# Late weights in 20 pieces behind the key quarters, and query transposes spread one by one, in a two-layer Perceiver kernel

## Chip, cores and metric

One core of one Trainium2 chip runs the whole program in one launch. The metric is the device time of that core in microseconds, the median of three runs. All engines of the core work side by side: PE (matrix products), DVE and ACT (vector and scalar work), POOL (small vector work), and SP, which here only issues DMAs.

## The reference, cut to what matters

The input is a sequence of 256 rows of 256 values and a context of 4096 rows. Two layers follow each other, each with a cross attention over the context, a self attention and a feed-forward part, every part added to x.

```python
x = x + L0_xattn(layernorm(x), ctx, ctx, mask)      # 16 heads of 16, tanh-capped scores
x = x + L0_attn(layernorm(x))                       # 16 heads
x = x + L0_ffn(layernorm(x))                        # quantised 256 x 256 product
x = x + L1_xattn(layernorm(x), ctx, ctx, mask1)     # 16 heads, q, k, v projected
x = x + L1_attn(layernorm(x))                       # causal, 16 heads of 64: Wq, Wk, Wv, proj
x = x + L1_ffn(layernorm(x))                        # attention, then a mixture of 8 experts
```

The change lies in the stage that computes the L0 feed-forward part and then the cross attention of layer 1. It moves the loads of the weights that `L1_attn` and the first half of `L1_ffn` use.

## The kernel before, in words

The program is four blocks one after the other: `stage_cross0`, `stage_self0`, `stage_cross1` and `stage_self1`. Inside a block every engine has its own stream of instructions, written out by hand, and the streams meet at semaphores. Between two blocks all engines meet at a barrier. No planner orders anything: the order of each stream is the order of the code.

**The head of `stage_cross1`.** DVE adds the last projection to x, normalises, and quantises the rows into `k.a_q` (the last of these steps is line 1656). PE first loads a register with the flag that says whether the second mask masks anything (line 1617, `pe.value_load`) and branches: the code of `all_heads(True)` lies ahead of that of `all_heads(False)`, and with these inputs the second is taken. `all_heads` starts with four dummy products (`keep_busy`, line 951), waits for `a_q`, transposes it (line 1542), and multiplies (line 941). Then come a second normalisation, the query projection, and the queries of all heads, split into three bf16 parts and stacked in rows (`k.q_rows1`).

**Query transposes and maxima.** The queries of heads 0 and 1 are transposed first (`turn_first`, line 1442). The others take four calls `turn(0)` to `turn(3)` (line 1453: 4 transposes in the first, 8 in each of the others), each followed by a copy on ACT into `k.q_all` (line 1402). Between them PE computes, for head 0, 16 products of 512 keys (`m_scores`, index `idx` 0 to 15, line 1476) into three PSUM banks in turn, and DVE reduces each to its maximum (line 1631): product n can only start when the reduction of product n - 3 has freed its bank. In the kernel before, `turn(0)` and `turn(1)` stand together behind `idx` 10, `turn(2)` and `turn(3)` behind `idx` 13. After `idx` 15 DVE takes the maximum over all (line 1635), POOL splits it (lines 1373 to 1379), PE turns it (line 1490), ACT copies it (line 1424), and the first product of the attention proper (line 1506) can start.

**Pairs of heads.** Then follow eight rounds of two heads. While head h is worked on, PE also computes the maxima of the next heads, and SP loads the keys of head h + 2 in quarters: four DMAs each (lines 1286 and 1287), as soon as the products of head h have read the quarter of that buffer. So `idx` 0, 4, 8 and 12 of a head are the first users of its four key quarters. SP does this in a loop, `sp.Fori(1, H // 2)`.

**Late weights.** `load_late_weights` (lines 1701 to 1721) issues 16 DMAs on SP at the very start of the block, ahead of the wait for `q_stack` and of that loop: three of 1 MB into `k.e_w`, one of 1 MB into `k.e_proj`, two small biases, one broadcast bias of 512 KB, and nine for the feed-forward part. They are needed in `stage_self1` only, where PE and DVE wait for `e_w_in` and `f_w_in`.

Of the kernel before, what the change touches and what calls it, by code (L numbers as in the profile page):

```python
# [27 lines left out]
P = 128  # L28
# [3 lines left out]
H = 16  # L32
DH = D // H
QT = S // P
KT = D // P
# [13 lines left out]
E_T = 8  # L49
E_DH = 64  # L50
N_EXP = 8
# [915 lines left out]
def update_dve(k, dve, link, tag, bias, turn, norm=True):  # L967

    v = k.nc.vector
    if turn:  # L970
        dve.wait_ge(k.sem(tag + "_oT_ps"), 1)
        v.tensor_copy(k.oT[:, :, :].rearrange("p c q -> p (c q)"), k.ps[:, 0, :]).then_inc(k.sem(tag + "_oT"), 1)
    if bias is not None:
        link(v.tensor_tensor(k.x[:, :, :], k.x[:, :, :], bias.unsqueeze(1).to_broadcast([P, QT, D]), ALU.add))
    dve.wait_ge(k.sem(tag + "_y"), 1)
    xf = k.x[:, :, :].rearrange("p t d -> p (t d)")
    link(v.tensor_tensor(xf, xf, k.ps[:, 1, :], ALU.add))
    if norm:
        layer_norm(k, dve, link, k.x, k.xn, k.sem(tag + "_xn"))
        dve.wait_ge(k.sem(tag + "_xnT_ps"), 1)  # L980
        v.tensor_copy(k.xnT[:, :, :].rearrange("p c q -> p (c q)"), k.ps[:, 2, :]).then_inc(k.sem(tag + "_xnT"), 1)
# [299 lines left out]
def load_k1_quarter(k, sp, h, b, quarter, loaded):  # L1281

    src = k.kd1[h, :, quarter * QUARTER:(quarter + 1) * QUARTER]
    dst = k.k_st[:, 2 * b + quarter // 2, quarter % 2 * QUARTER:(quarter % 2 + 1) * QUARTER]
    for r in range(PARTS):
        sp.dma_start(dst[2 * DH * r:2 * DH * (r + 1), :], src[0:2 * DH, :]).then_inc(loaded, 16)
    sp.dma_start(dst[LOROW:STACK, :], src[2 * DH:3 * DH, :]).then_inc(loaded, 16)


def stage_cross1(k):  # L1290
# [12 lines left out]
    s = {n: k.sem("d_" + n) for n in (  # L1303
        "scores", "exp", "pv", "q_staged", "v_staged", "m_scores", "m_read", "m_neg", "m_ops", "m_parts",
        "m_turned", "m_rows", "acc_copied", "sel", "rec", "o_read", "rows", "copies", "q_turned", "q_first", "q_stack")}
# [6 lines left out]
    def turned(n):  # L1312
        return k.ps[0:STACK, n, :].bitcast(BF16)
# [22 lines left out]
    with nc.Block() as block:  # L1336
        @block.sync
        def _(sp):
            def load_q(h, b):

                sp.dma_start(k.q_m[0:MAXROW, b, :], k.q_all[0:MAXROW, h, :]).then_inc(qm_in[b], 16)

            load_late_weights(k, sp)
            sp.wait_ge(s["q_stack"], H // 4)
            with sp.Fori(1, H // 2) as it:
                for b in range(2):

                    sp.wait_ge(s["m_read"], n_m * 2 * it + n_m * (b - 1))
                    load_q(2 * it + b, b)
                    for quarter in range(4):  # L1350
                        sp.wait_ge(s["scores"], 16 * it - 16 + 8 * b + 2 * (quarter + 1))
                        load_k1_quarter(k, sp, 2 * it + b, b, quarter, k_in[b][quarter])

        @block.gpsimd
        def _(pool):
# [79 lines left out]
        def _(pe):  # L1435
            t = nc.tensor
# [9 lines left out]
            def turn(n):  # L1446

                pe.wait_ge(s["copies"], 1)
                for h in range(4):
                    if 4 * n + h < 2:  # L1450
                        continue
                    for q in range(QT):
                        last = t.transpose(turned(n)[:, (h * QT + q) * P:(h * QT + q + 1) * P],
                                           k.q_rows1[:, FIRST_ROWS + q * (H - 2) + 4 * n + h - 2, :], k.ident_bf[:, :])
                last.then_inc(s["q_turned"], 1)
# [80 lines left out]
            def all_heads(masked):  # L1536
# [16 lines left out]
                turn_first()  # L1553
                for idx in range(n_m):
                    m_scores(0, 0, idx, masked, True, True)
                    if idx in (10, 13):
                        turn(2 * (idx // 3) - 6)
                        turn(2 * (idx // 3) - 5)
                for idx in range(M_AHEAD):
                    m_scores(0, 1, idx, masked, True, True)  # L1560
                pe.wait_ge(s["q_stack"], H // 4)
# [56 lines left out]
            with pe.If(masked):  # L1618
                all_heads(True)
            with pe.Else():  # L1620
                all_heads(False)
# [76 lines left out]
            normalise(H - 1, 1)  # L1698


def load_late_weights(k, sp):

    i = k.i
    done = k.sem("e_w_in")
    for n, name in enumerate(("Wq", "Wk", "Wv")):
        sp.dma_start(k.e_w[:, n], i[f"L1_attn_{name}T"].rearrange("(t p) n -> p t n", p=P)).then_inc(done, 16)
    sp.dma_start(k.e_proj, i["L1_attn_proj"].rearrange("(t p) n -> p t n", p=P)).then_inc(done, 16)
    sp.dma_start(k.e_bqk[:, 0, :], i["L1_attn_bq_cols"]).then_inc(done, 16)
    sp.dma_start(k.e_bqk[:, 1, :], i["L1_attn_bk_cols"]).then_inc(done, 16)
    sp.dma_start(k.e_bv, i["L1_attn_bv_row"].to_broadcast([P, 2 * E_T * E_DH])).then_inc(done, 16)  # L1710
    done = k.sem("f_w_in")
    sp.dma_start(k.f_wq, i["L1_ffn_WqT"].rearrange("(t p) n -> p t n", p=P)).then_inc(done, 16)
    sp.dma_start(k.f_wo, i["L1_ffn_WoT"].rearrange("(t p) n -> p t n", p=P)).then_inc(done, 16)
    for half in range(2):
        sp.dma_start(k.f_wkc[:, :, half * E_DH:(half + 1) * E_DH],
                     i["L1_ffn_WkcT"].rearrange("(t p) n -> p t n", p=P)).then_inc(done, 16)
    sp.dma_start(k.f_wvc, i["L1_ffn_WvcT"].rearrange("(t p) n -> p t n", p=P)).then_inc(done, 16)
    sp.dma_start(k.f_wr, i["L1_ffn_WrT"].rearrange("(t p) n -> p t n", p=P)).then_inc(done, 16)
    for n in range(2):
        sp.dma_start(k.f_g[:, n, :], i[f"L1_ffn_g{n + 1}_cols"]).then_inc(done, 16)  # L1720
    sp.dma_start(k.f_be, i["L1_ffn_expert_bias"].unsqueeze(0).to_broadcast([P, N_EXP])).then_inc(done, 16)


def rms_norm(k, dve, link, src, done):
# [19 lines left out]
def stage_self1(k):  # L1744

    nc, i = k.nc, k.i
    v, sc, t = nc.vector, nc.scalar, nc.tensor
    by_two = lambda heads: [((h, h + 1), q) for h in range(0, heads, 2) for q in range(QT)]
    half = lambda h: slice(E_DH * (h % 2), E_DH * (h % 2) + E_DH)
# [31 lines left out]
    with nc.Block() as block:  # L1781
# [27 lines left out]
        def _(pe):  # L1809
            update_pe(k, pe, "d", k.oT, KT, k.w1_o, True)  # L1810
            pe.wait_ge(k.sem("d_xnT"), 1)
            pe.wait_ge(k.sem("e_w_in"), 16 * 7)
            for n, (w, m) in enumerate(jobs):
                if n >= 4:
                    wait_evacuated(pe, n)
# [29 lines left out]
            pe.wait_ge(k.sem("f_xn"), QT)  # L1845
            transpose_rows(k, k.xn, 2, k.sem("f_xnT_ps"))
            pe.wait_ge(k.sem("f_xnT"), KT)
            pe.wait_ge(k.sem("f_w_in"), 16 * 9)
            for c in range(KT):
                last = t.matmul(k.ps[:, 5, 0:S], k.f_wkc[:, c, :], k.xnT[:, c, :], start=(c == 0), stop=(c == KT - 1))  # L1850
            last.then_inc(k.sem("f_proj"), 1)
# [88 lines left out]
        def _(dve):  # L1940
            link = Order(dve, k.sem("dve_order"), k.dve_ordered).link
            update_dve(k, dve, link, "d", k.b1_qo[:, 1, :], True)
            dve.wait_ge(k.sem("e_w_in"), 16 * 7)
            for n in by_dve:
                w, m = jobs[n]
                dve.wait_ge(k.sem("e_job"), n + 1)
# [25 lines left out]
            rsqrt(k, link, QT)  # L1972
            for q in range(QT):
                v.tensor_scalar(k.xn[:, q, :], k.x[:, q, :], k.ln_mv[:, q, 0:1], k.rs_y[:, q:q + 1], ALU.subtract, ALU.mult).then_inc(k.sem("f_xn"), 1)
            dve.wait_ge(k.sem("f_w_in"), 16 * 9)
            weigh_turned(k, dve, 0, k.sem("f_xnT_ps"), k.sem("f_xnT"))
            link(v.tensor_scalar(k.rs_v[:, 0:QT], k.ln_mv[:, :, 1], 1e-5, None, ALU.add))
            rsqrt(k, link, QT)
# [136 lines left out]
```

## Time and profile before

| what | value |
|---|---|
| median of 3 runs | 720.36 us (720.25 to 722.64) |
| profiled execution, span from first to last instruction | 715.4 us |
| PE busy | 612.3 us, 86% |
| ACT busy | 456.7 us, 64% |
| DVE busy | 407.2 us, 57% |
| POOL busy | 67.4 us, 9% |
| mean granted TensorE clock | 0.976 |

The profile gives the profiled execution's span, and no time of its own beyond it; the median stands 5.0 us above the span, for what lies around the first and the last instruction. PE is the busiest engine, but busy shares are an average over four stages with different limits. `stage_cross1` runs from 333.2 us to about 565 us of the span, and from 374 us on PE is busy almost without a gap.

### The profile page before, as it was taken

How to read it: one execution, taken by the hardware profiler on the slowest of the kernel's cores; microseconds unless marked ns; L12 is line 12 of the kernel's file. 1: busy time of each engine (PE TensorE's matmuls, PEld its weight loads, DVE VectorE, ACT ScalarE, POOL GpSimd, SP SyncE). 2: the span in 40 equal slices, each digit the busy share in tenths (PEclk: the TensorE clock that was granted, in tenths of full speed). 3: DMA queues.
4: the chain of work that ended last, by engine and by line, in shares of the span. 5: the costliest groups of instructions: out<-in, count | busy, mean ns of one | idle time of the engine just before them, and what ended most of it. 6: DMA issues, size and time to landing. Idle time of an engine off the chain costs nothing. (4 is left out here: it accounts for less than half of the span.)

```text
span 715.4 us, 14402 instructions
## 1 busy us (share of the span) xinstructions
PE 612.3 (86%) x4946; PEld 365.9 (51%) x4946; DVE 407.2 (57%) x899; ACT 456.7 (64%) x541; POOL 67.4 (9%) x151
## 2 busy tenths in 40 slices
PE   1698858878878879795679999999999999898998
PEld 0353424444444445463435555555555575574786
DVE  6567371322223134876389898989896226645644
ACT  3889969999999994683027676767676414603111
POOL 3000101100001100101031212121211000000000
PEclk9999989999999999999789999999999999999999
DMA  5786766556534313203602333332231390000000
GB/s 133 217 241 228 215 198 194 146 182 188 155 103 113 92 44 99 66 2 110 199 3 79 84 80 83 80 84 78 83 80 29 101 297 1 2 1 1 0 1 15
DMA packets 52832, 73.46 MB, mean 103 GB/s; under 512 B 10979, under 2 KB 29731, under 8 KB 52795
## 3 DMA queue, kind: packets, MB, share of 16 engines
q1 hardware_dynamic: 52027, 72.25, 34.8%
q10 hardware_dynamic: 768, 0.73, 0.4%
q8 instruction: 23, 0.38, 0.2%
q14 instruction: 14, 0.11, 0.1%
HBM read 58.90 MB, written 12.85 MB: 100 GB/s over the span
## 5 line engine op out<-in xcount | busy, mean ns | idle before, releaser
L1631 DVE TENSOR_REDUCE sb_m_blk<-ps 128x1 f32<-128x512 f32 x256 | 159.5, 684 | 18.9 <-PE ps L1476 17.7
L1412 ACT ACTIVATE sb_probs<-ps 128x1024 f32<-128x1024 f32 x128 | 125.8, 1024 | 50.0 <-PE ps L1506 49.7
L655 ACT ACTIVATE sb_probs<-ps 128x1024 f32<-128x1024 f32 x128 | 124.0, 1016 | 15.8 <-PE ps L701 13.4
L659 ACT ACTIVATE sb_probs<-sb_probs,sb_neg_cap,sb_cap 128x4096 f32<-128x4096 f32 x32 | 121.6, 3801 | 1.1
L718 PE MATMUL ps<-sb_probs,sb_v_st 128*32 128x256 f32 x1024 | 76.5, 395 | 39.5 <-ACT sb_probs L659 36.8
L701 PE MATMUL ps<-sb_q_st,sb_k_st 112*128 112x256 bf16 x512 | 75.7, 283 | 5.8 <-DMA sb_k_st<-k_parts_l 3.6
L1506 PE MATMUL ps<-sb_q_st,sb_k_st 115*128 115x256 bf16 x512 | 76.4, 272 | 1.5 <-ACT sb_probs L1412 1.5
L1476 PE MATMUL ps<-sb_k_st,sb_q_m 96*128 96x512 bf16 x224 | 76.6, 383 | 0.0
L701 PEld LDWEIGHTS ps<-sb_q_st,sb_k_st 112*128 112x128 bf16 x512 | 46.0, 100 | 48.9 <-ACT sb_probs L655 24.1
L1522 PE MATMUL ps<-sb_probs,sb_v_st 128*32 128x256 f32 x1024 | 67.4, 384 | 0.2 <-ACT sb_probs L1412 0.2
L718 PEld LDWEIGHTS ps<-sb_probs,sb_v_st 128*32 128x32 f32 x1024 | 24.0, 110 | 68.0 <-ACT sb_probs L659 45.0
L1506 PEld LDWEIGHTS ps<-sb_q_st,sb_k_st 115*128 115x128 bf16 x512 | 48.7, 97 | 18.0 <-issue 1.4
L1522 PEld LDWEIGHTS ps<-sb_probs,sb_v_st 128*32 128x32 f32 x1024 | 31.3, 109 | 27.3 <-issue 14.3
L951 PE MATMUL ps<-sb_w_o,sb_ones_sq 128*128 128x512 f32 (+1 forms) x82 | 35.3, 566 | 11.0 <-issue 11.0
L1082 ACT ACTIVATE sb_q_all<-ps,sb_nmax 128x256 f32<-128x256 f32 (+1 forms) x72 | 31.7, 452 | 12.1 <-DVE sb_nmax L1098 12.1
L1476 PEld LDWEIGHTS ps<-sb_k_st,sb_q_m 96*128 96x128 bf16 x224 | 22.7, 101 | 30.0 <-DVE sb_m_blk L1631 17.1
L613 POOL TENSOR_TENSOR sb_v_st<-sb_v_rows,sb_keep 128x512 f32<-128x512 f32 x14 | 14.9, 1065 | 210.8 <-PE ps L718 142.6
L861 DVE RECIPROCAL sb_rec<-ps 128x2 f32<-128x2 f32 x16 | 2.7, 170 | 51.5 <-PE ps L727 51.5
L855 DVE COPY sb_acc_sb<-ps 128x256 f32<-128x256 f32 x16 | 6.8, 423 | 41.5 <-PE ps L718 41.5
L1098 DVE TENSOR_REDUCE sb_nmax<-ps 128x2 f32<-128x512 f32 (+1 forms) x36 | 22.6, 631 | 13.5 <-PE ps L1021 7.2
L1073 ACT ACTIVATE sb_q_all<-ps 128x512 f32<-128x512 f32 (+1 forms) x36 | 19.8, 551 | 15.6 <-PE ps L1034 15.4
L1929 ACT ACTIVATE sb_probs<-ps 128x512 f32<-128x512 f32 x9 | 5.4, 597 | 36.9 <-PE ps L1887 36.9
(282 smaller groups left out, 824.0 us busy)
## 6 DMA issues: line engine op xcount, KB each, us to landing
sb_k_st<-k_parts_l SPq DMA_DIRECT2D x223, 64.0 KB, 2.0
sb_k_st<-k_parts_l SPq DMA_DIRECT2D x93, 128.0 KB, 3.2
k_parts_l<-sb_v_proj SPq DMA_DIRECT2D x24, 256.0 KB
k_parts_l<-sb_early SPq DMA_DIRECT2D x48, 128.0 KB
sb_v_proj<-ctxT_blocks SPq DMA_DIRECT2D x8, 512.0 KB, 8.4
sb_early<-ctxT SPq DMA_DIRECT2D x7, 512.0 KB, 3.8
sb_v_rows<-ctx_by_pair SPq DMA_DIRECT2D x7, 512.0 KB, 4.2
sb_k_st<-k_parts_l SPq DMA_DIRECT2D x64, 32.0 KB, 1.8
```

Source lines behind the costliest of these rows:

```text
L655: a.activation(probs[:, j % 2, 4 * g:4 * g + 4, :], scores_bank(g), ACT.Tanh).then_inc(s["tanh"], 1)
L659: a.activation(probs[:, j % 2], probs[:, j % 2], ACT.Exp, bias=k.neg_cap[:, 0:1], scale=k.cap[:, 0:1]).then_inc(s["exp"], 1)
L701: last = t.matmul(out[:, c, :], k.k_st[0:STACK0, j, n * P:(n + 1) * P], k.q_st[0:STACK0, j // 2, :], start=True, stop=True)
L718: last = t.matmul(k.ps[32 * m:32 * m + 32, 4 + b, 0:S], k.v_st[:, b, (j % 2) * UNIT_CH + ch, :], probs[:, j % 2, ch, :], start=(j % 2 == 0 ...
L951: k.nc.tensor.matmul(k.ps[:, bank, 0:cols], k.ones_sq[:, :], k.w1_o[:, :, :].rearrange("p t n -> p (t n)")[:, 0:cols], start=True, stop=True)
L1082: sc.activation(k.sp_rows[:, n % 2, e, 0:nk], a.scores(n)[:, e, 0:nk], ACT.Exp, bias=k.nmax[:, 2 * n + e:2 * n + e + 1], accum_out=k.sums[ ...
L1098: v.tensor_reduce(k.nmax[:, 2 * n:2 * n + 2], a.scores(n)[:, :, 0:nk], AX.X, ALU.max, negate=True).then_inc(s["max"], 1)
L1412: sc.activation(probs[:, g], scores_bank(g), ACT.Exp).then_inc(s["exp"], 1)
L1476: last = t.matmul(o, qs[0:MAXROW, b, q * P:(q + 1) * P], k.k_st[0:MAXROW, 2 * b + blk // (m_blocks // 2), key0:key0 + 512], start=True, st ...
L1506: last = t.matmul(out[:, c, :], k.k_st[0:STACK, j, ch * P:(ch + 1) * P], k.q_st[0:STACK, b, :], start=True, stop=not masked)
L1522: last = t.matmul(k.ps[32 * m:32 * m + 32, ACC_BANK, 0:S], k.v_st[:, b, GROUP_CH * g + m, :], probs[:, g, m, :], start=(g == 0), stop=(g = ...
L1631: v.tensor_reduce(k.m_blk[:, b, q, blk:blk + 1], k.ps[:, m_bank(m_turn_of(idx)), :], AX.X, ALU.max).then_inc(s["m_read"], 1)
```

## The change

The late weights are no longer issued at the head of the block. A list of 20 loads is made instead (the three 1 MB weights in two halves each, `proj` in two halves, the others as before), and SP issues one of them behind each key quarter of the rounds 1, 2 and 3 of the loop over pairs of heads: 8 in the first, 8 in the second, 4 in the third. These three rounds are written out, and the loop runs over rounds 4 to 7. The waits count 11 and 9 loads instead of 7 and 9. On PE the four calls of `turn` stand one each behind `idx` 11, 12, 13 and 14.

```diff
-            load_late_weights(k, sp)
-            sp.wait_ge(s["q_stack"], H // 4)
-            with sp.Fori(1, H // 2) as it:
+            def keys_of_pair(it, late=()):
                 for b in range(2):
 
                     sp.wait_ge(s["m_read"], n_m * 2 * it + n_m * (b - 1))
...
                         load_k1_quarter(k, sp, 2 * it + b, b, quarter, k_in[b][quarter])
+                        for load in late[4 * b + quarter:4 * b + quarter + 1]:
+                            load()
+
+            sp.wait_ge(s["q_stack"], H // 4)
+            weights = late_weights(k, sp)
+            for it in range(1, 4):
+                keys_of_pair(it, weights[8 * (it - 1):8 * it])
+            with sp.Fori(4, H // 2) as it:
+                keys_of_pair(it)
...
                     m_scores(0, 0, idx, masked, True, True)
-                    if idx in (10, 13):
-                        turn(2 * (idx // 3) - 6)
-                        turn(2 * (idx // 3) - 5)
+                    if 11 <= idx < 11 + H // 4:
+                        turn(idx - 11)
...
+    loads = []
     for n, name in enumerate(("Wq", "Wk", "Wv")):
...
+        w = i[f"L1_attn_{name}T"].rearrange("(t p) n -> p t n", p=P)
+        loads += [load(k.e_w[:, n, t], w[:, t], "e_w_in") for t in range(KT)]
+    proj = i["L1_attn_proj"].rearrange("(t p) n -> p t n", p=P)
+    loads += [load(k.e_proj[:, n:n + 4], proj[:, n:n + 4], "e_w_in") for n in (0, 4)]
+    loads += [load(k.e_bqk[:, n, :], i[f"L1_attn_{name}_cols"], "e_w_in") for n, name in enumerate(("bq", "bk"))]
+    loads.append(load(k.e_bv, i["L1_attn_bv_row"].to_broadcast([P, 2 * E_T * E_DH]), "e_w_in"))
...
-            pe.wait_ge(k.sem("e_w_in"), 16 * 7)
+            pe.wait_ge(k.sem("e_w_in"), 16 * E_LOADS)
```

## Rows read from the trace of the kernel before

**Rows 1.** The page's head and its busy times: share, instructions.

```profile
span 715.4 us, 14402 instructions
PE 612.3 (86%) x4946; PEld 365.9 (51%) x4946; DVE 407.2 (57%) x899; ACT 456.7 (64%) x541; POOL 67.4 (9%) x151
```

**Rows 2.** Waits of PE over the whole span: us, times, longest.

```profile
PE ps L951 <- issue: 11.0, 2, 7.7
```

**Rows 3.** Timeline of PE around the block's start: start, us, what, [idle before].

```profile
330.93 2.00 PE L941 MATMUL ps<-sb_early,sb_oT 128*128 128x256 f32 x8 [0.80 <-DVE sb_oT L1259]
340.62 2.50 PE L951 MATMUL ps<-sb_w_o,sb_ones_sq 128*128 128x256 f32 x5 [7.70 <-issue]
346.43 1.44 PE L951 MATMUL ps<-sb_w_o,sb_ones_sq 128*128 128x256 f32 x3 [3.31 <-issue]
...
347.24 0.15 PEld L1542 LDWEIGHTS ps<-sb_ident_bf,sb_a_q 128*128 128x128 bf16 x1
```

**Rows 4.** Timeline of DVE in the same stretch.

```profile
340.38 0.43 DVE L1656 TENSOR_SCALAR sb_a_q<-sb_ctx_two 128x512 bf16<-128x512 f32 x1
348.33 0.42 DVE L1658 COPY sb_a_qT<-ps 128x512 bf16<-128x512 bf16 x1 [7.53 <-PE ps L1542]
```

**Rows 5.** Timeline of SP's DMA issues; 16 late loads lie between first and last.

```profile
333.21 0.40 SPq L1706 DMA_DIRECT2D sb_early<-L_attn_WqT  x1
...
335.46 5.72 SPq L1708 DMA_DIRECT2D sb_e_bqk<-L_attn_bq_cols  x1
...
348.85 0.43 SPq L1721 DMA_DIRECT2D sb_v_rows<-L_ffn_expert_bias  x1
```

**Rows 6.** Instruction queue: whole span, then 337.9:338.3, 343.7:344.1, 349.0:349.4; packets, MB, share.

```profile
q8 instruction: 23, 0.38, 0.2%
...
q8 instruction: 1, 0.02, 15.3%
...
q8 instruction: 1, 0.02, 17.5%
...
q8 instruction: 1, 0.02, 20.5%
```

**Rows 7.** Windows: us, busy of PE, PEld, DVE, ACT, POOL, clock, DMA share, GB/s.

```profile
336.00:341.00 5.00, 0.38 (x1) 0.38 (x2) 4.38 (x15) 0.00 (x0) 0.54 (x1) 0.55 1.03 414
344.00:347.00 3.00, 0.57 (x2) 0.48 (x2) 0.00 (x0) 0.00 (x0) 0.00 (x0) 0.50 1.07 336
374.00:398.00 24.00, 23.41 (x233) 13.33 (x234) 21.83 (x39) 17.03 (x20) 3.02 (x12) 1.00 0.28 78
```

**Rows 8.** Key loads, issue to landing in us: whole span, then 378:380.

```profile
sb_k_st<-k_parts_l SPq DMA_DIRECT2D x223, 64.0 KB, 2.0
sb_k_st<-k_parts_l SPq DMA_DIRECT2D x64, 32.0 KB, 1.8
...
sb_k_st<-k_parts_l SPq DMA_DIRECT2D x1, 64.0 KB, 3.1
```

**Rows 9.** Timeline of PE and DVE around the four `turn` calls.

```profile
366.05 1.21 PE L1476 MATMUL ps<-sb_k_st,sb_q_st 96*128 96x512 bf16 x2
367.05 1.49 PE L1453 MATMUL ps<-sb_ident_bf,sb_v_rows 128*115 128x128 bf16 x12
369.61 1.57 PE L1453 MATMUL ps<-sb_ident_bf,sb_v_rows 128*115 128x128 bf16 x16
371.01 0.60 PE L1476 MATMUL ps<-sb_k_st,sb_q_st 96*128 96x512 bf16 x2
...
369.00 1.89 DVE L1631 TENSOR_REDUCE sb_m_blk<-ps 128x1 f32<-128x512 f32 x3 [0.62 <-PE ps L1476]
371.43 1.29 DVE L1631 TENSOR_REDUCE sb_m_blk<-ps 128x1 f32<-128x512 f32 x2 [0.55 <-PE ps L1476]
```

**Rows 10.** Timeline of the first round: SP's key issues, PE's first uses of quarters 1, 2.

```profile
382.27 0.32 SPq L1287 DMA_DIRECT2D sb_k_st<-k_parts_l  x1
382.84 1.25 SPq L1286 DMA_DIRECT2D sb_k_st<-k_parts_l  x3
384.27 0.32 SPq L1287 DMA_DIRECT2D sb_k_st<-k_parts_l  x1
...
386.38 0.39 PE L1476 MATMUL ps<-sb_k_st,sb_q_m 96*128 96x512 bf16 x1
388.30 0.38 PE L1476 MATMUL ps<-sb_k_st,sb_q_m 96*128 96x512 bf16 x1
```

More of the change, by code:

```diff
@@ L1698, in _, with late_weights, load @@
             normalise(H - 1, 1)
-def load_late_weights(k, sp):
+E_LOADS = 11
+F_LOADS = 9
+def late_weights(k, sp):
     i = k.i
-    done = k.sem("e_w_in")
+    def load(dst, src, sem):
+        return lambda: sp.dma_start(dst, src).then_inc(k.sem(sem), 16)
+    loads = []
     for n, name in enumerate(("Wq", "Wk", "Wv")):
[L1706 to L1721, printed above, removed]
@@ new lines, in late_weights @@
+    assert len(loads) == E_LOADS
+    for dst, name in ((k.f_wq, "WqT"), (k.f_wo, "WoT"), (k.f_wkc[:, :, 0:E_DH], "WkcT"), (k.f_wkc[:, :, E_DH:2 * E_DH], "WkcT"),
+                      (k.f_wvc, "WvcT"), (k.f_wr, "WrT")):
+        loads.append(load(dst, i["L1_ffn_" + name].rearrange("(t p) n -> p t n", p=P), "f_w_in"))
+    loads += [load(k.f_g[:, n, :], i[f"L1_ffn_g{n + 1}_cols"], "f_w_in") for n in range(2)]
+    loads.append(load(k.f_be, i["L1_ffn_expert_bias"].unsqueeze(0).to_broadcast([P, N_EXP]), "f_w_in"))
@@ L1724, in rms_norm @@
+    assert len(loads) == E_LOADS + F_LOADS
+    return loads
 def rms_norm(k, dve, link, src, done):
@@ L1847, in _ @@
             pe.wait_ge(k.sem("f_xnT"), KT)
-            pe.wait_ge(k.sem("f_w_in"), 16 * 9)
+            pe.wait_ge(k.sem("f_w_in"), 16 * F_LOADS)
             for c in range(KT):
@@ L1942, in _ @@
             update_dve(k, dve, link, "d", k.b1_qo[:, 1, :], True)
-            dve.wait_ge(k.sem("e_w_in"), 16 * 7)
+            dve.wait_ge(k.sem("e_w_in"), 16 * E_LOADS)
             for n in by_dve:
@@ L1974, in _ @@
                 v.tensor_scalar(k.xn[:, q, :], k.x[:, q, :], k.ln_mv[:, q, 0:1], k.rs_y[:, q:q + 1], ALU.subtract, ALU.mult).then_inc(k.sem("f_xn"), 1)
-            dve.wait_ge(k.sem("f_w_in"), 16 * 9)
+            dve.wait_ge(k.sem("f_w_in"), 16 * F_LOADS)
             weigh_turned(k, dve, 0, k.sem("f_xnT_ps"), k.sem("f_xnT"))
```

## Prediction

> **What bounds the kernel now.** I read the page first: PE is busy 86% of a span of 715.4 us [rows 1], so whatever the change gives back must lie in PE's gaps or move the chain that feeds it. The waits of PE come next. Most of its idle time is ended by ACT or DVE; one entry is not: line 951, dummy products that wait for no data, was preceded by 11.0 us of idle ended by "issue" [rows 2], in two gaps, 7.70 us ahead of 340.62 and 3.31 us ahead of 346.43 [rows 3]. Nothing that the profile shows held PE there. It had no instructions.
>
> The DMA view says why. The instruction queue moves pieces of 16 KB (23 in the span, 0.38 MB) and one starts at about 338.1, one at 343.9, one at 349.2 [rows 6]. PE runs 2.5 us after the start of each of the first two (340.62, 346.43) [rows 3, 6]. So PE, which has jumped over the code of the masked case, waits for its first piece, works through the few instructions of it that lie behind the branch's target (five products), and waits again for the second. In the same stretch the 16 DMA engines are full: share 1.03 and 1.07, 414 and 336 GB/s [rows 7], all of it the late weights, which SP issues from 333.21 to 349.3 [rows 5]. The granted clock is 0.50 to 0.55 there, after PE had been idle [rows 7].
>
> Does the gap lie on the path? DVE has `a_q` ready at 340.38 + 0.43 = 340.81; PE begins to transpose it at 347.24, and DVE gets it back at 348.33 after 7.53 us of idle [rows 3, 4]. So 347.24 - 340.81 = 6.4 us of the span are lost to missing code. The first 7.5 us of PE's idle time lie under DVE's normalisation and cost nothing alone.
>
> **The change, part by part.**
>
> 1. *The 16 late loads leave the head of the block.* SP has nothing else to do there before 372, so its own time is no gain. What changes is how long a code piece takes. With the queue full: the second piece is wanted, at the latest, when PE starts on the first, 340.62, and starts to move at 343.9, 3.3 us later. Put the same 3.3 us ahead of the first one and it was asked for at 334.8, 1.6 us after the block's start, which leaves room for the register load and the branch. From asking to running: 3.3 + 2.5 = 5.8 us, of which the transfer itself is about 1.0 us (15.3% of 16 engines in 0.4 us) [rows 6].
>  With an empty queue no row shows it. The nearest rows are key loads at a DMA share of 0.28: 1.8 and 2.0 us from issue to landing, and 3.1 us for one in the first round [rows 7, 8]. Now it is 3.3 + 1.0 = 4.3 us to landing. I take 2.2 us, a little over the median of 223 loads, since the piece is one packet of 1 us on one engine where a key load is cut over many. That is 2.1 us less for each of two pieces, 4.2 us in sum. Check by the clock: first piece running at 334.8 + 2.2 + 1.5 = 338.5, second at 338.5 + 2.2 + 1.5 = 342.2 (the five products take until 341.0), three more dummy products of 0.8 us, transposes at 343.0 against 347.24, and `a_q` long there. Bounds: landing after 1.8 us gives 5.0, after 3.1 us gives 2.4. Above, DVE caps the gain at 6.4; below, it is nothing if the 4.3 us are the piece's own time and not the queue's. I take 4.2.
>
>  The trace's two stalls are both at code pieces, yet 21 other pieces cost PE nothing visible [rows 2, 6]. The Trainium skill, "Runtime: NRT & Kernel Launch", section "Instruction fetch mechanics", says that a taken branch to a target outside the window forces a fetch before execution goes on, and that crossing from one 16 KB block to the next is mostly hidden. The trace agrees on the branch (7.70 us) and not on the crossing right behind it (3.31 us); if only full queues caused that second stall, the gain would be the whole 6.4, which is a rival below.
>
> 2. *Twenty loads go behind key quarters.* SP's stream: an issue costs 0.4 to 0.5 us for a large load [rows 5]. In the first round SP has 382.84 - 382.59 = 0.25 us between two quarters [rows 10], so each slot sets it back by some 0.2 us, 0.6 us by the fourth; it catches up at the next head's first quarter, which waits for PE. (The 5.72 us of the fifth load [rows 5] came behind 4 MB in flight; here at most half a MB is.) The DMA engines: a 512 KB piece at 414 GB/s is 1.27 us [rows 7]; the key quarter behind it lands up to that much later. Who waits: `idx` 4 at 386.38 for the quarter issued by 382.59, which lands 1.8 us later at 384.4, a slack of 2.0; `idx` 8 at 388.30 for that issued by 384.59, landed 386.4, a slack of 1.9 [rows 8, 10]. Against it stand 1.27 + 0.4 = 1.7 us. It just holds. From the second head on the slack is wider, because quarter and use are a whole head apart. DMA share rises from 0.28 to under 0.7. Cost 0; bounds 0 and 1 us (five heads by 0.2). PE's code pieces of this stretch are fetched ahead and would have to be late by a piece's whole run to count. SP's written-out rounds are straight code of a few hundred instructions; 0. In `stage_self1` the weights have been there for over 100 us; 0.
>
> 3. *One transpose call at a time.* From 366.64 to 371.61 PE is full: 28 transposes in 1.49 + 1.57 us and five products of 512 keys; DVE idles 0.62 and 0.55 us for want of products [rows 9]. The same work in another order: `idx` 11 must wait for the bank of `idx` 8, free at about 367.13, so PE loses some 0.1 us; then each call of 0.8 us fits beside the 0.62 us reductions with two or three products in hand, and only the last two leave DVE gaps. The last product starts at about 371.3 and DVE ends near 372.4 instead of 371.43 + 1.29 = 372.72. Gain 0.3 us, and it is on the path, for maximum, split and first score follow from it. Bounds: 1.2 us gained (both gaps gone), 0.3 lost (PE's work just ends later). The copies on ACT come in earlier and end before the split does; 0.
>
> Sum: 4.2 + 0.3 = 4.5 us off the span, 715.4 to 710.9, and with the 5.0 us between span and median, 720.36 - 4.5 = **715.9 us**.
>
> **Rivals.**
>
> A, the forecast: both pieces come faster, neither is hidden. For it: the stall coincides to the microsecond with full engines. 715.9 us, own range 714 to 718.3.
>
> B, *the code fetch is slow by itself.* The pieces need their 4.3 us on empty queues too; only the 0.3 us of part 3 is left, 720.1 us. For it: a packet of 16 KB is not larger on a full engine (1.0 us), and code queue and load queue are different queues, so the fetch might never have stood behind the weights. Against it: three starts are 5.8 and 5.3 us apart under load, and a 64 KB load lands in 2.0 us without. Beside it, the Trainium skill, "DMA: Bandwidth & Descriptors", section "Queues, rings and completion order", says that an engine takes turns between queues packet by packet; with the 4 KB rows of the weights that would mean a wait of a fraction of a microsecond, and so would speak for B. No row here shows it.
>
> C, *the second stall vanishes,* because the second piece arrives while the first one's five products run, and PE is ready before DVE: 6.4 + 0.3 = 6.7, 713.7 us. Against it: the second piece moved only 5.8 us after the first, as if asked for late.
>
> D, slower: *the weights starve the keys.* Place: the wait for key quarters 1 to 3 in round 1. It decides once a piece sets back the quarter behind it by over 1.9 us. From then on every later slot puts at least SP's 0.45 us on the path: 17 slots x 0.45 = 7.7, less 4.5, gives 723.5 us. For it: margins of 0.2 us. Against it: quarters are issued on PE's progress, so slack comes back.
>
> **How the numbers follow.** A 0.67, B 0.15, C 0.12, D 0.06. No change, to half a per cent (3.6 us, about what a measurement can tell), takes in B and the part of A in which a fetch lands after 2.7 us or more, some 0.2. So faster 0.61, same 0.34, slower 0.05. The range goes from 713.0 (beyond C) to 720.3 (B in it), and leaves out D and the tails.
>
> **What would show it.** Right: the idle ended by "issue" ahead of line 951 falls from 11.0 to near 7 us; the transposes of line 1542 start near 343; DVE's wait ahead of line 1658 falls from 7.53 to about 3.3; the DMA share between 334 and 350 is near 0 and between 377 and 430 over 0.5; PE stays full from 374 on. Wrong: PE's two gaps unchanged (B), a wait for `sb_k_st` in PE's list (D), or a wait at line 1820 for late weights.

## The result and the profile after

The changed kernel takes 716.26 us, the median of 6 runs (713.8 to 718.55). Six runs of the kernel before beside them gave 721.86 us (720.25 to 723.89). The ratio is 0.9919, 95% interval 0.9891 to 0.9948, which is 5.6 us off. A second measurement (the last experiment below) gave 717.16 against 721.9, 0.9946 [0.9913, 0.9979]. One of all the runs reported below took 808 us at a mean clock of 0.75, and the ratios leave it out. The profiled execution after took 713.8 us, its span 711.3. Its page and its waits of PE begin so, against 715.4 us and 11.0 us of "issue" before [rows 1, 2]:

```profile
span 711.3 us, 14227 instructions
PE 614.1 (86%) x4946; PEld 366.0 (51%) x4946; DVE 407.2 (57%) x899; ACT 457.2 (64%) x541; POOL 67.9 (10%) x151
```

```profile
PE ps L951 <- issue: 5.6, 2, 4.7
...
PE ps L1483 <- DVE sb_m_blk L1637: 3.4, 8, 1.0
```

PE is as busy as before; 5.4 us of gaps ahead of line 951 have gone. The changed file is six or seven lines longer there: L1476, L1542, L1631 and L1658 of before are L1483, L1549, L1637 and L1664. The timeline of PE at the head of the block answers to [rows 3]:

```profile
331.34 1.99 PE L941 MATMUL ps<-sb_early,sb_oT 128*128 128x256 f32 x8 [0.81 <-DVE sb_oT L1259]
338.06 2.35 PE L951 MATMUL ps<-sb_w_o,sb_ones_sq 128*128 128x256 f32 x5 [4.73 <-issue]
341.27 1.44 PE L951 MATMUL ps<-sb_w_o,sb_ones_sq 128*128 128x256 f32 x3 [0.87 <-issue]
342.51 0.63 PE L1549 MATMUL ps<-sb_ident_bf,sb_a_q 128*128 128x128 bf16 x4
```

The first gap has shrunk from 7.70 to 4.73 us, the second from 3.31 to 0.87. The weight load of the first transpose starts at 342.08 and its product at 342.51, where 347.24 and 347.67 stood; the block itself starts 0.4 us later here, so that is 5.6 us. The timeline of DVE [rows 4, 9]:

```profile
340.79 0.43 DVE L1662 TENSOR_SCALAR sb_a_q<-sb_ctx_two 128x512 bf16<-128x512 f32 x1
343.18 0.42 DVE L1664 COPY sb_a_qT<-ps 128x512 bf16<-128x512 bf16 x1 [1.96 <-PE ps L1549]
...
356.36 8.06 DVE L1637 TENSOR_REDUCE sb_m_blk<-ps 128x1 f32<-128x512 f32 x13 [0.89 <-PE ps L1483]
364.87 0.69 DVE L1637 TENSOR_REDUCE sb_m_blk<-ps 128x1 f32<-128x512 f32 x1 [0.45 <-PE ps L1483]
365.94 1.36 DVE L1637 TENSOR_REDUCE sb_m_blk<-ps 128x1 f32<-128x512 f32 x2 [0.37 <-PE ps L1483]
```

DVE waits 1.96 us for the transposes instead of 7.53: 5.6 us. From its first reduction to the last one's end pass 10.9 us, against 11.2 before.

The DMA view of two stretches of 0.6 us, 335.4 to 336.0 and 338.4 to 339.0, in 40 slices each, shows where a code piece begins to move [rows 6]:

```profile
DMA  0000000000900000000000000000000000000000
...
DMA  0000000000000000000000900000000000000000
```

One starts at 335.4 + 10 x 0.015 = 335.55, the other at 338.73. PE runs 2.5 us behind each start (338.06, 341.27), as before (338.1 and 340.62, 343.9 and 346.43). So a piece that has begun to move is no faster. It begins to move sooner: after PE's last product (333.33) in 2.2 us instead of 5.2, and after PE's start on the piece before (338.06) in 0.7 us instead of 3.3. That is 3.0 + 2.6 = 5.6 us.

The windows answer to [rows 7]:

```profile
336.00:341.00 5.00, 2.35 (x5) 1.71 (x6) 4.58 (x16) 0.00 (x0) 0.95 (x2) 0.72 0.01 3
344.00:347.00 3.00, 3.00 (x10) 1.53 (x9) 2.04 (x7) 0.00 (x0) 0.00 (x0) 0.82 0.01 3
...
378.00:384.00 6.00, 6.00 (x63) 3.42 (x65) 4.78 (x9) 4.49 (x7) 1.61 (x5) 1.00 0.95 279
384.00:396.00 12.00, 10.97 (x113) 6.17 (x105) 10.36 (x19) 8.36 (x11) 1.81 (x6) 1.00 1.06 243
```

The DMA share at the head is 0.01 instead of 1.03. In the first round it is 0.95 and 1.06, more than the "under 0.7" of the prediction, and between 384 and 396 PE is short of 1.03 us of work. The gap, in the timelines of PE and of DVE:

```profile
393.60 0.90 PE L1483 MATMUL ps<-sb_k_st,sb_q_m 96*128 96x512 bf16 x3
394.34 0.60 PE L1513 MATMUL ps<-sb_q_st,sb_k_st 115*128 115x256 bf16 x4
395.97 0.39 PE L1483 MATMUL ps<-sb_k_st,sb_q_m 96*128 96x512 bf16 x1 [1.03 <-DVE sb_m_blk L1637]
399.14 0.66 PE L1483 MATMUL ps<-sb_k_st,sb_q_m 96*128 96x512 bf16 x2 [0.15 <-DVE sb_m_blk L1637]
```

```profile
393.37 2.54 DVE L1637 TENSOR_REDUCE sb_m_blk<-ps 128x1 f32<-128x512 f32 x4 [1.22 <-PE ps L1483]
```

The profile names DVE, and this is a label to distrust. The product at 395.97 is `idx` 8 of head 3 and needs the bank of `idx` 5, whose reduction ended at about 393.37 + 1.27 = 394.6; PE was ready at 394.94. What came last is its other wait, the third key quarter. The last part of that quarter was issued at 389.32. The DMA view of 387.9 to 389.5 and then of 391 to 396, median us from issue to landing at the end of a line:

```profile
sb_k_st<-k_parts_l SPq DMA_DIRECT2D x1, 32.0 KB, 6.5
...
sb_early<-L_attn_proj SPq DMA_DIRECT2D x2, 512.0 KB, 7.1
sb_k_st<-k_parts_l SPq DMA_DIRECT2D x6, 64.0 KB, 4.7
sb_k_st<-k_parts_l SPq DMA_DIRECT2D x1, 32.0 KB, 6.3
```

389.32 + 6.5 = 395.8, just ahead of the product. Key loads land after 4.7 and 6.3 to 6.5 us where they took 2.0 and 1.8 [rows 8]. Together the two gaps lose 1.2 us. Two experiments below show the same stall with its DMA named.

### The profile page after: what moved, and what is told of

It is laid out like the page before. It is cut to its first block and busy times, and to the rows that moved or that the text cites. A ratio compares the mean times of both kernels' runs of the same rounds, so it can differ in the third digit from the quotient of the medians.

```text
span 711.3 us, 14227 instructions
## 1 busy us (share of the span) xinstructions
PE 614.1 (86%) x4946; PEld 366.0 (51%) x4946; DVE 407.2 (57%) x899; ACT 457.2 (64%) x541; POOL 67.9 (10%) x151
## 5 line engine op out<-in xcount | busy, mean ns | idle before, releaser
L1637 DVE TENSOR_REDUCE sb_m_blk<-ps 128x1 f32<-128x512 f32 x256 | 159.7, 685 | 19.6 <-PE ps L1483 18.3
L1483 PE MATMUL ps<-sb_k_st,sb_q_m 96*128 96x512 bf16 x224 | 76.7, 383 | 1.2 <-DVE sb_m_blk L1637 1.2
L1483 PEld LDWEIGHTS ps<-sb_k_st,sb_q_m 96*128 96x128 bf16 x224 | 22.7, 101 | 31.4 <-DVE sb_m_blk L1637 18.6
L750 PE MATMUL ps<-sb_early 128*128 128x512 f32 x56 | 29.2, 649 | 0.0
```

The costliest lines, as they stand in the source:

```text
L750: last = t.matmul(k.ps[:, bank, :], k.wk1[:, c, j * P:(j + 1) * P], ctx[:, c, :], start=(c == 0), stop=(c == KT - 1))
L1483: last = t.matmul(o, qs[0:MAXROW, b, q * P:(q + 1) * P], k.k_st[0:MAXROW, 2 * b + blk // (m_blocks // 2), key0:key0 + 512], start=True, st ...
L1637: v.tensor_reduce(k.m_blk[:, b, q, blk:blk + 1], k.ps[:, m_bank(m_turn_of(idx)), :], AX.X, ALU.max).then_inc(s["m_read"], 1)
```

## The experiments

**Where the time goes by stage.** Times are from DVE's first instruction of the block (`sb_x<-sb_x,ps`, 333.65 after), read from the timelines. "Pairs" is from the first score product to the next block's first transposes. One profile each; no row holds for more than its own execution. Where no key is late, "pairs" is 190.0 at a mean clock of 1.00 and 191.3 to 191.5 with a half-clock period inside it; after has 191.49 at 1.00, and that is the late keys' work.

| kernel | `a_qT` copied | first reduction | reductions to maximum | first score | pairs |
|---|---|---|---|---|---|
| before | 15.08 | 28.26 | 11.25 | 41.83 | 190.02 |
| after | 9.53 | 22.71 | 10.97 | 36.01 | 191.49 |
| after, again | 9.86 | 23.83 | 11.52 | 37.67 | 193.00 |
| loads only | 9.28 | 22.04 | 10.67 | 35.03 | 190.44 |
| turns only | 15.29 | 28.47 | 10.93 | 41.72 | 189.99 |
| turns only, again | 15.98 | 29.81 | 11.43 | 43.57 | 191.49 |
| loads in the gap | 9.85 | 23.45 | 11.34 | 37.24 | 191.38 |
| no branch | 8.26 | 23.03 | 10.67 | 36.02 | 189.99 |
| every other quarter | 9.67 | 23.22 | 11.31 | 37.00 | 191.35 |
| the same, old turns | 9.25 | 23.08 | 11.65 | 37.21 | 191.32 |
| 1 KB rows | 15.54 | 29.55 | 11.65 | 43.55 | 191.47 |
| two dummy products | 11.68 | 24.86 | 10.90 | 38.08 | 189.99 |
| five dummy products | 8.05 | 20.81 | 11.13 | 34.43 | 191.25 |
| 1 MB at the head | 11.74 | 26.09 | 10.45 | 38.87 | 189.99 |

**1. The loads alone.** The changed kernel with the old order of the transposes.

```diff
-                    if 11 <= idx < 11 + H // 4:
-                        turn(idx - 11)
+                    if idx in (10, 13):
+                        turn(2 * (idx // 3) - 6)
+                        turn(2 * (idx // 3) - 5)
```

> The changed kernel with the old places of the four turn calls (two behind idx 10, two behind idx 13), the late loads as changed. Theory (queue): the loads alone carry the gain at the head of the block, so from the end of a_q to its copy from PSUM it takes about 2.4 us instead of 7.9, PE's issue gaps ahead of line 951 stay at 4.7 and 0.9 us, and only the stretch from the first to the last reduction of head 0's maxima is 0.3 us longer than changed (11.25 against 10.97 us). Total 0.3 us above the changed kernel, about 5 us below before. Rival (the order of the transposes matters more than the loads): total within 1 us of before.

Measured: 715.51 us, ratio 0.9914 [0.9876, 0.9953], as much as the whole change. Two waits of PE:

```profile
PE ps L951 <- issue: 5.2, 2, 4.9
...
PE ps L1483 <- DMA sb_k_st<-k_parts_l: 0.3, 1, 0.3
```

The gain is the loads'. Here the profile names the key load as what ended PE's wait in head 3, 0.3 us of it.

**2. The turns alone,** measured on two chips. The kernel before with the diff of experiment 1 the other way round.

> The kernel before with only the four turn calls moved. Theory: gaps of 7.7 and 3.3 us ahead of line 951 unchanged, 0.3 us gained in the stretch of the reductions (11.25 to 10.97 us); total 0.3 us below before, which the timing can't tell from nothing. Rival (the moved calls help the clock or the copies): over 1 us.

> The same kernel as e2 once more, with more rounds, since its time came out 3 us below before while its profile showed 0.1 us. Theory (no effect of the turn calls): ratio to before within 0.998 and 1.002. Rival (a real effect outside the stretch looked at): 0.996 again.

Measured: 720.03 us, 0.9958 [0.9924, 0.9991]; then 722.64 us, 1.0023 [0.9989, 1.0056]. The second takes back what the first seemed to show. The "issue" idle stays, at 11.2 us (7.7 and 3.5) in the first profile and 11.9 us (7.6 and 4.3) in the second. The stretch from the first reduction to the maximum took 10.93 and 11.43 us, against 11.25. The same pair is in experiment 5: the new order at 718.12 us, the old at 718.2. The turns do nothing that can be measured.

**3. All 20 loads in the gap.** They go behind the transposes of `a_q` (the semaphore `c_aqT_ps`), where PE has its code and no key is due.

```diff
-            def keys_of_pair(it, late=()):
+            sp.wait_ge(k.sem("c_aqT_ps"), 1)
+            for load in late_weights(k, sp):
+                load()
+            sp.wait_ge(s["q_stack"], H // 4)
+            with sp.Fori(1, H // 2) as it:
...
-                        for load in late[4 * b + quarter:4 * b + quarter + 1]:
-                            load()
...
```

> The changed kernel, but the 20 late loads go all together behind the transposes of a_q (SP waits for c_aqT_ps), into the stretch in which the DMA engines idle, about 344 to 361 us; the key loop is the old one. Theory (weights starve the keys of head 3): PE's waits at line 1483 of 1.03 and 0.15 us near 395 and 399 go, as in the kernel before, and the gaps at the head stay at 4.7 and 0.9 us: 1.2 us below the changed kernel, about 6.5 below before. Rival (those waits are for the PSUM banks and have nothing to do with the weights): the same 1.2 us of waits, total as changed. Second rival: a later code piece of PE stands behind the weights and PE stops for 1 to 4 us between 346 and 372.

Measured: 717.0 us, 0.9898 [0.985, 0.9946]. The gaps are 5.03 and 0.74 us, and PE waits for no key. So the gain needs no place in the key rounds; it is enough that the head is free. The profiled execution was the longest of the four (720.0 us), at a mean clock of 0.967 against 0.978 after.

**4. No branch.** The kernel before with its 16 loads at the head, and PE without the test of `masked`.

```diff
-            masked = pe.value_load(k.masked_i[0:1, 0:1], min_val=0, max_val=1)
-            with pe.If(masked):
-                all_heads(True)
-            with pe.Else():
-                all_heads(False)
+            all_heads(False)
```

> The kernel before without the register load and the branch: only the unmasked code is in the program (it leaves out the masked case), and the 16 late loads stay at the head of the block. Theory (PE lacks code because its jump throws away what was fetched ahead, and the new pieces stand behind the weights): no gap ended by issue ahead of line 951, a_q transposed at once: 6.4 us below before although the DMA engines are just as full. Rival (full DMA engines slow PE down in another way, or the stall comes from the barrier): gaps of several us remain, total within 2 us of before.

Measured: 715.47 us, 0.9902 [0.9864, 0.9941]. The timeline of PE, and the window 334 to 350:

```profile
332.74 1.97 PE L951 MATMUL ps<-sb_w_o,sb_ones_sq 128*128 128x256 f32 x8 [0.32 <-PEq L1129]
340.36 0.61 PE L1542 MATMUL ps<-sb_ident_bf,sb_a_q 128*128 128x128 bf16 x4 [5.65 <-DVE sb_a_q L1652]
342.31 6.58 PE L951 MATMUL ps<-sb_w_o,sb_ones_sq 128*128 128x512 f32 x10
```

```profile
334.00:350.00 16.00, 9.15 (x26) 4.21 (x24) 10.94 (x41) 0.00 (x0) 1.91 (x4) 0.79 0.97 338
```

Not one gap by "issue" is left, while the DMA engines are as full as before (0.97). Both are needed for the stall: a taken branch, and full engines to make it long. One limit: between 322 and 361 us this kernel moves no 16 KB code piece at all, so it does not show what a piece in straight code costs on full engines. The changed kernel does. The instruction queue in its DMA view of 389.4 to 389.8:

```profile
q8 instruction: 1, 0.02, 20.3%
```

One piece moves there, in the stretch with a share of 1.06, and no idle time of PE's products between 386 and 400 is ended by "issue". In the kernel without the branch PE is ready long ahead of DVE, idles 5.65 us, and then works at a lower granted clock (0.67 between 342 and 349): ten dummy products take 6.58 us where they took 4.75 at 0.94 after the change. Part of the gain is given back there (first reduction at 23.03, not earlier than with the branch and free engines).

**5. Half the rate.** One piece behind every other quarter, over rounds 1 to 5; once with the new order of the turns, once with the old.

```diff
-                        for load in late[4 * b + quarter:4 * b + quarter + 1]:
-                            load()
+                        if quarter % 2 == 0:
+                            for load in late[2 * b + quarter // 2:2 * b + quarter // 2 + 1]:
+                                load()
...
-            for it in range(1, 4):
-                keys_of_pair(it, weights[8 * (it - 1):8 * it])
-            with sp.Fori(4, H // 2) as it:
+            for it in range(1, 6):
+                keys_of_pair(it, weights[4 * (it - 1):4 * it])
+            with sp.Fori(6, H // 2) as it:
```

> The changed kernel with the 20 pieces behind every second key quarter of five rounds instead of every quarter of three. Theory (the keys of head 3 land late because a 512 KB piece behind every quarter fills the DMA engines, and the delay adds up from quarter to quarter): DMA share of the first round falls from 0.82 to about 0.6, no wait at line 1483 for a late key quarter in rounds 1 to 5, the stretch from the first score to the block's end goes back from 191.5 to 190.0 us; total 1.2 to 1.5 us below the changed kernel. Rival (one piece ahead of a quarter is enough to make it late): waits remain, up to five rounds of them, total as changed or worse.

> As e4, and the four turn calls in their old places. Theory (the order of the turn calls is worth nothing that lasts; what moved in that stretch by 0.3 us either way is where a half-clock period falls): within 0.5 us of e4, reductions of head 0 take between 10.7 and 11.3 us in both. Rival (one at a time is worth its 0.3 us): e4's stretch is shorter by 0.3 us.

Measured: 718.12 us (12 runs, with the one at 808 us; 717.68 without it), 0.9934 [0.9901, 0.9966], and 718.2 us, 0.9948 [0.9917, 0.9979]. Windows of the first:

```profile
372.00:378.00 6.00, 5.89 (x38) 3.14 (x39) 4.57 (x8) 3.07 (x4) 0.00 (x0) 0.72 0.08 24
378.00:384.00 6.00, 6.00 (x60) 3.30 (x62) 5.96 (x11) 4.80 (x5) 1.20 (x5) 1.00 0.63 181
384.00:396.00 12.00, 12.00 (x122) 6.80 (x118) 10.44 (x20) 8.42 (x11) 1.80 (x6) 1.00 0.60 179
```

The share is 0.60 instead of 1.06, PE is full from 378 to 396, and neither profile has a wait for a key left. The stall was the weights' doing. The time is no better for it: 1.2 us is less than the spread of the runs (713.8 to 718.55 for the changed kernel). The first window shows one reason. Its clock is 0.72: a half-clock period has fallen into the first round, where it costs PE about 1.3 us (pairs 191.35 against 190.0), and in other executions it falls elsewhere.

**6. Rows of 1 KB.** The three big weights' places are filled by loads with 1 KB rows (those of `proj`) instead of 4 KB at the head; the true loads follow behind the transposes.

```diff
+            for n in range(3):
+                sp.dma_start(k.e_w[:, n].rearrange("p t n -> p (t n)").rearrange("p (t n) -> p t n", n=D),
+                             k.i["L1_attn_proj"].rearrange("(t p) n -> p t n", p=P)).then_inc(filled, 16)
...
+            sp.wait_ge(k.sem("c_aqT_ps"), 1)
             load_late_weights(k, sp)
```

> The kernel before, but what stands at the head of the block is 4 MB in rows of 1 KB (the attention projection, once to its place and three times into the place of Wq, Wk and Wv as a filler), and the real loads follow behind the transposes of a_q. In the kernel before, three of the 4 MB come in rows of 4 KB. Theory (a code piece takes its turn with the weights' queue packet by packet, so its delay goes with the size of the rows ahead): the DMA engines are as full, but the gaps ahead of line 951 shrink from 7.7 and 3.3 us to near those of the changed kernel, under 6 and under 2 us. Rival (it stands behind the bytes already queued, whatever their rows): gaps of 7 to 8 and 3 us as before.

Measured: 727.29 us in one run at a mean clock of 0.960. The timeline of PE, and the packets of 336 to 348:

```profile
345.02 2.50 PE L951 MATMUL ps<-sb_w_o,sb_ones_sq 128*128 128x256 f32 x5 [7.88 <-issue]
351.11 1.44 PE L951 MATMUL ps<-sb_w_o,sb_ones_sq 128*128 128x256 f32 x3 [3.59 <-issue]
```

```profile
DMA packets 3117, 3.16 MB, mean 264 GB/s; under 512 B 43, under 2 KB 3116, under 8 KB 3116
```

Rows a quarter as long, and the same stall (one profile). This is what the rival of the expectation said, gaps of 7 to 8 and 3 us. The Trainium skill, "DMA: Bandwidth & Descriptors", section "Queues, rings and completion order", has an engine take turns packet by packet, a packet there being typically 9 to 17 descriptors. If each row is one descriptor, that is an estimated 1.4 to 2.7 us with 4 KB rows, at 0.16 us a row (414 GB/s over 16 engines [rows 7]), and about a quarter of it with 1 KB rows. By that alone the stall would have shortened with the rows, and here it did not. The first piece is the clean case (7.88 against 7.70 us); by the time of the second, the kernel before has rows of 1 KB in flight too, those of its own `proj`.

The bytes fit better. What the DMA engines moved from PE's first product of the first piece to the start of the second piece, in the kernel before (340.62 to 343.94) and here (345.02 to 348.73):

```profile
DMA packets 664, 1.31 MB, mean 393 GB/s; under 512 B 16, under 2 KB 459, under 8 KB 663
...
DMA packets 1281, 1.31 MB, mean 352 GB/s; under 512 B 20, under 2 KB 1280, under 8 KB 1280
```

The same 1.31 MB goes ahead of the second piece, in 664 packets before (459 of them under 2 KB) and in 1281 here; in the two profiles of experiment 2 it is 1.28 and 1.60 MB. Ahead of the first piece the loads had moved 1.30 MB before and 1.19 MB here. That fits the rival's reason too, a piece that stands behind bytes already queued. No run varies that amount for itself, so it is not shown, and what the piece waits for stays open.

**7. 1 MB at the head.** The kernel before, with `WqT` at the head and the other 15 loads behind the transposes.

```diff
         sp.dma_start(k.e_w[:, n], i[f"L1_attn_{name}T"].rearrange("(t p) n -> p t n", p=P)).then_inc(done, 16)
+        if n == 0:
+            sp.wait_ge(k.sem("c_aqT_ps"), 1)
```

> The kernel before with only the first load (1 MB, Wq) at the head of the block and the other 15 behind the transposes of a_q. Theory (a code piece waits for what is queued on the DMA engines ahead of it): 1 MB is through by about 337, so the first gap is 5 to 7 us instead of 7.7, the second is 0.7 to 1 us as in the changed kernel. Rival (any load in flight costs the full 3 us each): gaps of 7.7 and 3.3 us as before.

Measured: 719.81 us in one run at a clock of 0.969. The timeline of PE, and the windows 337 to 340 and 340 to 344:

```profile
342.82 2.50 PE L951 MATMUL ps<-sb_w_o,sb_ones_sq 128*128 128x256 f32 x5 [7.09 <-issue]
345.89 1.44 PE L951 MATMUL ps<-sb_w_o,sb_ones_sq 128*128 128x256 f32 x3 [0.57 <-issue]
```

```profile
337.00:340.00 3.00, 0.00 (x0) 0.00 (x0) 2.72 (x13) 0.00 (x0) 2.22 (x4) 0.81 0.98 313
340.00:344.00 4.00, 1.18 (x3) 1.00 (x4) 3.32 (x10) 0.00 (x0) 0.00 (x0) 0.50 0.10 36
```

The engines are full for 3 us and then nearly free (share 0.10). The first piece is wanted in the full part and PE's gap is 7.09 us, just beyond the 5 to 7 expected; the second finds them free, 0.57 us. The first begins to move at 340.38, when the loads have moved 1.04 MB, nearly all of the 1 MB (1.05 million bytes); the expectation had that through by "about 337", and it took until 340.4 in a block that starts at 336.05. In one kernel both cases stand side by side (one profile): what counts is whether the engines are full when the piece is wanted.

**8. Work for PE ahead of the branch.** The kernel of experiment 5 (new turns) with two, then five dummy products more, placed ahead of the branch to keep the clock up while the code comes. Each is two matmul records in the trace, four and ten in all; the products counted from here on are records.

```diff
+            keep_busy(k, 5, 6)
             masked = pe.value_load(k.masked_i[0:1, 0:1], min_val=0, max_val=1)
```

> The kernel of e4 with two more dummy products of 512 columns on PE ahead of the register load and the branch, so that the array works for 1.7 us while the sequencer jumps. Theory (PE's idle of 4.7 us behind the branch is what lets the granted clock fall to a half around the copy of a_q, and later steps pay for it): the half-clock stretch at the head gets shorter or goes, copy of xnT at +15.6 instead of +16.8 us after the block's start, total 1 to 2 us below e4. Rival (the dummies hold the branch up, since PE's sequencer gets past them only when the array has room): the code pieces are asked for up to 1.7 us later, and a_q's copy comes that much later.

> As e8, with five products, 4.4 us of array time. Theory: clock stays full at the head; if the sequencer runs past all of them, a_q's copy is at +9.6 us as in e4 and total 2 to 3 us below e4. Rival: the branch waits for the queue to drain, a_q's copy at +11 to +13 us, total 1 to 3 us above e4.

Measured: two products 714.66 us, 0.9906 [0.9872, 0.9939]; five products 713.58 us, 0.9883 [0.9835, 0.9932]. The timeline of PE with two:

```profile
336.28 0.48 PE L951 MATMUL ps<-sb_w_o,sb_ones_sq 128*128 128x256 f32 x1 [2.62 <-issue]
339.77 3.14 PE L951 MATMUL ps<-sb_w_o,sb_ones_sq 128*128 128x256 f32 x7 [3.01 <-issue]
```

and with five, with the window 336 to 341:

```profile
332.16 4.53 PE L951 MATMUL ps<-sb_w_o,sb_ones_sq 128*128 128x512 f32 x10 [0.32 <-PEq L1129]
336.94 1.99 PE L951 MATMUL ps<-sb_w_o,sb_ones_sq 128*128 128x256 f32 x8 [0.25 <-issue]
339.78 0.40 PE L1550 MATMUL ps<-sb_ident_bf,sb_a_q 128*128 128x128 bf16 x4 [0.84 <-DVE sb_a_q L1664]
```

```profile
336.00:341.00 5.00, 3.38 (x17) 1.95 (x16) 4.00 (x12) 0.00 (x0) 0.00 (x0) 1.00 0.01 3
```

The added instructions also move the code behind them. With two (four records), one product instead of five is left of the piece into which the branch jumps, and PE waits 3.01 us for the next, on empty engines; the copy of `a_qT` comes 2.0 us later than in experiment 5, as late as the rival said, but for this reason: the first piece begins to move 2.3 us behind PE's last product of the block before, in both kernels. With five, eight products follow without a gap and the transposes wait for DVE, the clock at 1.00 in this window; the copy comes at 8.05 us, earlier than either expectation.

The second stall can be added up. In the eight profiles that have it on free engines the second piece begins to move about 0.7 us after PE's first product of the first (338.06 to 338.73 after the change, 336.28 to 336.95 with two), and runs 2.2 to 2.8 us later. So PE stops for about 3.2 us less what is left to do in the first piece: 2.35 us leave 0.87, 0.48 us leave 3.0.

On one chip five products gave 713.58 us against 717.16 for the changed kernel; all six runs lie below that median, though the intervals against the kernel before overlap, and this kernel also has the half rate of experiment 5. This is the best version measured. How much of it is the clock and how much the place of the branch's target was not separated. The fit in the last section, which takes the clock out, leaves 1.9 (0.9) and 3.0 us (1.1) for the two kernels of this experiment, no more than for the change, so what they have over it goes with their clock (0.979 on average).

**9. The changed kernel again,** beside experiments 7 and 8.

> The changed kernel once more, beside e8 and e9 on one chip. Theory (5.8 us gained at the head, 1.2 us given back to late keys of the second round's head 3, the rest is the clock): ratio to before 0.992 to 0.995, a wait of 0.5 to 1.5 us at line 1483 behind a late key quarter once more. Rival (the waits for keys were an accident of one execution): none this time.

Measured: 717.16 us (12 runs), 0.9946 [0.9913, 0.9979]. PE's waits, and one line of its timeline:

```profile
PE ps L951 <- issue: 5.8, 2, 5.1
...
PE ps L1483 <- DMA sb_k_st<-k_parts_l: 0.6, 1, 0.6
```

```profile
396.46 0.39 PE L1483 MATMUL ps<-sb_k_st,sb_q_m 96*128 96x512 bf16 x1 [0.65 <-DMA sb_k_st<-k_parts_l]
```

The same two facts once more: shorter code gaps, and a stall for a key quarter in head 3.

## Why the prediction was right, and where it was off

**Direction, cause and total** held: 716.26 us against 715.9 predicted, 5.6 us off where 4.5 were worked out. That the total came within 0.4 us is partly luck: six runs put the kernel before at 721.86 us and not at 720.36, and in the profile two errors cancel, 1.4 us too little at the head (part 1) and 1.5 us too little lost in the pairs (part 2). The cause was code pieces that PE lacked behind its taken branch, made late by the weights. The loads alone give the gain, the turns alone give none. Without the branch the stall disappears; without the loads it shrinks by half.

**Part 1, the code pieces: mechanism right, size too small.** "That is 2.1 us less for each of two pieces, 4.2 us in sum" should read 3.0 + 2.6 = 5.6. The step that failed is "I take 2.2 us" to landing, with 1.5 us more to running: 3.7 us from wanting to running. Measured for the second piece: 0.7 + 2.5 = 3.2 us; for the first, counted from the same 1.9 us behind PE's last product: 4.73 - 1.87 = 2.9 us. The median of key loads on lightly used engines was not the near row that I took it for: idle engines took a code piece up sooner. Even the upper bound of 5.0 (landing after 1.8 us) was too low. That a piece runs 2.5 us after it begins to move, full engines or not, was right to 0.1 us; when the first piece was asked for, no view shows.

**Part 2, the keys: cost 0 was wrong, the bound of 1 us nearly right.** Head 2, which the prediction checked to a few tenths, holds. "From the second head on the slack is wider, because quarter and use are a whole head apart" is the step that failed. The trace of the kernel before has the last part of head 3's third quarter issued at 395.64 and its first user, `idx` 8, at 400.20:

```profile
395.64 0.32 SPq L1287 DMA_DIRECT2D sb_k_st<-k_parts_l  x1
...
400.20 0.38 PE L1476 MATMUL ps<-sb_k_st,sb_q_m 96*128 96x512 bf16 x1
```

That is 4.6 us, with 1.8 us to landing a slack of 2.8, where a head takes 12. And each piece was priced as a delay of its own that ends before the next. But eight pieces of 512 KB and the keys fill the engines entirely (share 1.06), what is left over is passed on, and the landing time of the pieces grows from 4.2 (`WqT`) over 5.5 and 6.5 to 7.1 us (`proj`). The third and fourth quarters of head 3 (first used by `idx` 8 and 12) meet the sum of it: 1.2 us in the first profile, 0.6 and 0.3 in two others.

**Part 3, the turns: 0.3 us, not found.** The stretch took 10.45 to 11.65 us in the profiles with the old order and 10.90 to 11.52 in those with the new one, so its order is lost in the scatter. DVE's gaps merely moved: 0.45 and 0.37 us instead of 0.62 and 0.55.

**Sum.** 5.6 at the head, about 0.3 in the stretch, less 1.5 in the pairs: the block ends 4.35 us sooner in the profiled execution, and the span falls by 4.1. The medians fell by 5.6 and 4.7. The 0.3 is no larger than the scatter of that stretch.

**The rivals.** B (the fetch is slow by itself) is refuted: gaps 5.6 us instead of 11.0. It was not all wrong: on idle engines the branch still costs PE 4.7 us, most of it under DVE's normalisation. Its "fraction of a microsecond" took one row of 4 KB for a packet; by the section named in experiment 6 a packet is more. C (the second stall vanishes) is nearly what happened, 0.87 us left of 3.31; the reason against it, that the second piece is asked for late, was drawn from a time at which the queue itself was late. D (the keys starve) has its mechanism and its place, the late quarters of round 1 (there at head 3, whose keys that round loads), but not its price: the slots did not add up, for the quarters follow PE's progress, as the prediction argued against it.

**The signs.** "Issue" fell to 5.6, below the 7 foretold; the transposes started at 342.1 (343); DVE's wait is 1.96 (3.3); the DMA share 0.01 (0). The sign "over 0.5" between 377 and 430 was met (0.71) and told too little, for the 12 us in which the share was 1.06 hold the stall. "PE stays full from 374 on" failed, and the wait for `sb_k_st` that was to speak for D stands in PE's list in two other profiles.

## What to carry to other kernels

Idle time that is ended by "issue", with no releaser, right behind a taken branch, was missing code here: look at the instruction queue and at what else fills the DMA engines at that moment, and move bulk loads away from the branch or take out the branch. Loads that are slipped in between others must be summed over the whole stretch, not priced one by one; at a share near 1 the delays were passed on, and the later quarters paid. And a gain of under 1% needs many runs and stage times from the trace, because the span of one profile against another holds the clock's scatter as well.

## What the hardware did that was not expected

- From the start of a code piece's transfer to PE's first instruction of it pass 2.5 us in both kernels (2.2 to 2.8 in the other profiles), on full and on free engines alike; only the start moved, by 3.0 and 2.6 us. Neither 1 KB rows in place of 4 KB (gaps of 7.88 and 3.59 us) nor, for the first piece, 1 MB in place of 3 and more (7.09 us) brings much of that back.
- The second stall goes with what is left of the piece behind the branch's target, even on free engines: 0.3 to 0.9 us with five products (records) left, 3.0 us with one, none with eight. The Trainium skill, "Runtime: NRT & Kernel Launch", section "Instruction fetch mechanics", calls the step from one block of code to the next mostly hidden. The traces agree in straight code (21 other pieces, one of them on full engines, experiment 4) and not right behind a taken branch.
- The scatter from run to run goes with the granted clock. 64 runs of the kernel before, on three chips, took on average 726.8 us at a mean clock of 0.960, 721.6 at 0.969 and 717.3 at 0.976, some 5 to 6 us for each 0.01. That is as much as the change brings. A fit over all runs of the kernels, with one slope for the clock and a step for each kernel, gives 3.5 us (plus or minus 0.6) for the change, 4.3 (1.1) for the loads alone, and 0.4 and 0.0 (0.8 and 0.7) for the turns alone. The rest of the difference, 1.5 us, is a slightly higher clock (means 0.9716 and 0.9687), whose cause was not tried.
